# A two-layer graph network: layer 1 computed as (scaled h)ᵀ·adjᵀ first and W last

## The reference

```python
h = relu(layernorm(x))
# layer 0: attention over adj, three powers
Xw = h @ Wv + bv;  sj = Xw @ aw[:d, 0];  si = Xw @ aw[d:, 0]
e = leaky_relu(sj[:, None, :] + si[:, :, None] + ab[0], 0.2)
alpha = adj * exp(e);  T = alpha / (sum(alpha, -1) + 1e-12)
H = sum_k ((T^k h) @ Wk[k] + bk[k]),  k = 0, 1, 2
x = x + relu(H)
# layer 1
h = relu(layernorm(x))
Ah = adj + eye;  dh = rsqrt(sum(Ah, -1))
x = x + relu((dh * Ah * dh) @ h @ W + bias)
```

## Time and profile before

| | us |
|---|---|
| median of 3 runs | 801.88 (801.55 to 802.0) |
| the profiled execution | 801.45 |
| its span | 799.5 |
| TensorE busy | 784.4 (98%) |
| VectorE busy | 638.6 (80%) |
| ScalarE busy | 515.5 (64%) |
| GpSimd busy | 129.4 (16%) |
| granted TensorE clock | 0.998 of full |

### The profile page before, as it was taken

How to read it: one execution, slowest core, us unless ns; L and a number is a source line. 1 busy time by engine, 2 the same in 40 slices (tenths; PEclk the granted TensorE clock), 3 DMA queues, 4 the chain that set the end, 5 groups by cost and what they waited for, 6 DMA issues and landing times.

```text
span 799.5 us, 15983 instructions
## 1 busy us (share of the span) xinstructions
PE 784.4 (98%) x6142; PEld 756.0 (95%) x6142; DVE 638.6 (80%) x1544; ACT 515.5 (64%) x987; POOL 129.4 (16%) x120
## 2 busy tenths in 40 slices
PE   8798999999999999999999999999999999999998
PEld 8597999989999899998999999999999999999998
DVE  6985889868897688976989679896798868895676
ACT  3986766757576676666667567665776657667142
POOL 1032010311104111030201402023010220103200
PEclk9999999999999999999999999999999999999999
DMA  7555435843278251772527625284343842356403
GB/s 240 221 156 170 139 117 177 274 144 134 66 224 295 75 171 54 244 258 67 194 70 250 214 73 192 75 297 156 126 140 128 287 127 99 100 182 234 158 9 106
DMA packets 64492, 128.71 MB, mean 161 GB/s; under 512 B 5536, under 2 KB 31520, under 8 KB 64416
## 3 DMA queue, kind: packets, MB, share of 16 engines
q1 hardware_dynamic: 55648, 97.01, 37.1%
q10 hardware_dynamic: 8768, 30.68, 11.5%
HBM read 119.28 MB, written 8.39 MB: 160 GB/s over the span
## 4 chain that ended last, share of the span: by engine, by line
PE 91%; ACT 4%; DVE 4%; issue 1%; DMA 0%; POOL 0%; SPq 0%; DVEq 0%; ACTq 0%
PE acc L1029 22%; PE acc L1031 22%; PE acc L1030 22%; PE da L904 13%; PE db L904 6%; PE tp L896 3%; ACT tg_e L393 1%; PE acc L924 1%; ACT t_hi L407 1%; ACT tg_e L399 1%; DVE h L587 1%; DMA h<-x_dram 0%; DVE g_tmp L677 0%; DVE ht_lo L606 0%; ACT a_raw L424 0%
## 5 line engine op out<-in xcount | busy, mean ns | idle before, releaser
L1029 PE MATMUL acc<-g_hi,t_hi 128*128 128x256 f32 (+1 forms) x1024 | 293.0, 286 | 2.7 <-DVE g_lo L632 2.7
L1031 PE MATMUL acc<-g_hi,t_lo 128*128 128x256 f32 (+1 forms) x1024 | 289.9, 283 | 0.0
L1030 PE MATMUL acc<-g_lo,t_hi 128*128 128x256 f32 x1024 | 288.7, 282 | 0.0
L1029 PEld LDWEIGHTS acc<-g_hi,t_hi 128*128 128x128 f32 x1024 | 193.9, 189 | 3.1 <-issue 3.1
L1030 PEld LDWEIGHTS acc<-g_lo,t_hi 128*128 128x128 f32 x1024 | 194.3, 190 | 0.0
L1031 PEld LDWEIGHTS acc<-g_hi,t_lo 128*128 128x128 f32 x1024 | 194.1, 190 | 0.0
L1029 PE MATMUL acc<-g_hi,a_hi 128*128 128x256 f32 x512 | 145.5, 284 | 0.1
L1030 PE MATMUL acc<-g_lo,a_hi 128*128 128x256 f32 x512 | 144.0, 281 | 0.0
L1031 PE MATMUL acc<-g_hi,a_lo 128*128 128x256 f32 x512 | 144.0, 281 | 0.0
L327 POOL TENSOR_TENSOR g_lo<-g_tmp,g_hi 128x256 fp32r<-128x256 f32 x64 | 60.6, 947 | 353.0 <-ACT g_hi L449 353.0
L393 ACT ACTIVATE tg_e<-si,sij 128x256 f32<-128x256 f32 x256 | 109.4, 501 | 12.9 <-DVE t_lo L657 10.2
(11 more groups left out here) (129 smaller groups left out, 1424.3 us busy)
## 6 DMA issues: line engine op xcount, KB each, us to landing
a_raw<-adj_dram SPq DMA_DIRECT2D x64, 512.0 KB, 4.5
a_raw<-adj_t_dram SPq DMA_DIRECT2D x64, 512.0 KB, 4.9
tg_a<-adj_t_dram ACTq DMA_DIRECT2D x58, 512.0 KB, 4.0
x_res<-x_dram SPq DMA_DIRECT2D x64, 128.0 KB, 3.6
out_dram<-o_tile SPq DMA_DIRECT2D x64, 128.0 KB, 3.0
...
```

Source lines behind the costliest of these rows:

```text
L1029: nc.tensor.matmul(acc[:, s, 0:n], l_hi, r_hi, start=(jt == 0), stop=False)
L1030: nc.tensor.matmul(acc[:, s, 0:D], l_hi, r_lo, start=False, stop=False)
L1031: ins = nc.tensor.matmul(acc[:, s, 0:n], l_lo, r_hi, start=False, stop=(jt == NT - 1))
```

## The change

Layer 1 is computed in the other order. The normalised h is scaled by dh first (the factor goes into the power: GpSimd takes ((var + eps) · row sum)^(-1/2), `moments1`), and `hs_high` on ScalarE applies it, with a bias that VectorE makes (`bias1_of`) and relu, into `tmp`, and rounds it to `hs_hi`; `hs_low` on VectorE makes the low part. The tiles of hs are the weights as they lie, so nothing is transposed, and the adjacency moves, 512 columns at a time: `layer1_piece(q)` is six matmuls of 512 columns that add tile q mod 8 of h into the transposed sum of half of the rows, (`zt[0]` for q = 0 to 7, in the banks of `da`; `zt[1]` for q = 8 to 15, in those of `tp`). A second array, `adj_z`, has the adjacency in that order; a chunk of it serves two pieces. When eight pieces are summed, zt is split (`zt_high`, `zt_low`, into `ht_hi` and `ht_lo`) and is the weights of the product with W, `out_product`, six matmuls of 256 columns for each tile of rows; `out_chunk` on VectorE finishes it straight from that bank. Products 0 to 3 stand behind pieces 10 to 13, products 4 to 7 behind chunks 1 to 4 of the next batch's U (in the last batch at its end).

Besides: the norm of layer 0 moves from VectorE to ScalarE (`norm0`, with `bias0`), h of a batch is loaded in four parts, each once the pieces no longer read the space it shares with `hs_hi`, the diagonal is two instructions for each of four chunks instead of one for each of eight, and the tables of T's units are new.

```diff
-    LEAKY_Z, EXP_Z = {0: 5, 4: 6, 6: 7}, {0: 5, 5: 6, 6: 7}
-    HIGH_Z, HIGH_U = {3: 4, 5: 5}, {0: 6, 1: 7}
+    LOW_V = {1: 0, 2: 1, 6: 2}
+    LEAKY_Z, EXP_Z = {3: 5, 6: 6, 11: 7}, {4: 5, 7: 6, 12: 7}
+    HIGH_Z, HIGH_U = {0: 3, 5: 4, 9: 5, 13: 6}, {0: 7}
...
+    OUT_Z = {10 + i: i for i in range(HJ)}
+    OUT_U = {1 + i: HJ + i for i in range(HJ)}
...
+            def load_h0(b, g):
+                if b > 1:
+                    sp.wait_ge(piece_done, (b - 2) * NP + NT + 2 * g + 2)
+                else:
+                    sp.wait_ge(tp0_full, NG)
+                sp.dma_start(h0[:, 2 * g:2 * g + 2, :], x_v[b, :, 2 * g:2 * g + 2]).then_inc(x0_loaded[g], 16)
...
+            def hs_high(b, par, g):
+                act.wait_ge(nb1_ready, b * NG + g + 1)
+                if g > 0:
+                    act.wait_ge(hs_ready, b * NT + 2 * g)
+                for t in (2 * g, 2 * g + 1):
+                    nc.scalar.activation(tmp[:, t % 2, :], p0[:, par, t, :], ACT.Relu, bias=nb1[:, t:t + 1],
+                                         scale=rstd1[:, t:t + 1]).then_inc(h1_ready, 1)
+                for t in (2 * g, 2 * g + 1):
+                    act.wait_ge(h1_ready, b * NT + t + 1)
+                    nc.scalar.copy(hs_hi[:, t, :], tmp[:, t % 2, :]).then_inc(hs_hi_done, 1)
+            def zt_high(b, r):
+                for f in range(KD):
+                    if f == KD - 1:
+                        act.wait_ge(piece_done, b * NP + (r + 1) * NT)
+                    else:
+                        act.wait_ge(zt_full, 2 * b + r + 1)
+                    nc.scalar.copy(zt_hi[:, f, :], zt[r][:, f, :]).then_inc(zt_hi_done, 1)
...
-                    l1_scaled(b, 2 * g)
-                    l1_scaled(b, 2 * g + 1)
-                        a_round(b, *A_FIRST[i])
...
+                for q in range(NP):
+                    if q == NP // 2:
+                        zt_high(b, 0)
+                    if q + 4 < NP:
+                        a_round(b, (q + 4) // 2, q % 2)
+                    if q == 1:
+                        hs_high(b, par, NG - 1)
+                    if not last:
+                        if q in HIGH_Z:
+                            t_high(b + 1, HIGH_Z[q], b + 2 == B)
+                        if q in LEAKY_Z:
+                            leaky(b + 1, LEAKY_Z[q])
+                        if q in EXP_Z:
+                            exponent(b + 1, EXP_Z[q])
...
+                nc.vector.scalar_tensor_tensor(out=ve1[:, c], in0=mv1[:, c, 1], scalar=EPS_LN, in1=row_a1[:, c],
+                                               op0=ALU.add, op1=ALU.mult).then_inc(ve1_ready, 1)
...
+            def hs_low(b, g):
+                for t in (2 * g, 2 * g + 1):
+                    dve.wait_ge(hs_hi_done, b * NT + t + 1)
+                    nc.vector.tensor_tensor(hs_lo[:, t, :], tmp[:, t % 2, :], hs_hi[:, t, :].bitcast(F32),
+                                            ALU.subtract).then_inc(hs_ready, 1)
+            def zt_low(b, r):
+                for f in range(KD):
+                    dve.wait_ge(zt_hi_done, (2 * b + r) * KD + f + 1)
+                    nc.vector.tensor_tensor(zt_lo[:, f, :], zt[r][:, f, :], zt_hi[:, f, :].bitcast(F32),
+                                            ALU.subtract).then_inc(zt_ready, 1)
+            def out_chunk(b, par, i):
                 s = i % 2
 
-                dve.wait_ge(acc_full, b * PHASES + 2 * NT + i + 1)
-                nc.vector.scalar_tensor_tensor(out=z_tmp[:, s, :], in0=acc[:, acc_slot(Z_PHASE, i), 0:D], scalar=dh[:, i:i + 1],
+                dve.wait_ge(out_full, b * NT + i + 1)
+                if i == 0:
+                    dve.wait_ge(dh_ready, b + 1)
+                dve.wait_ge(stored[s], 16 * (b * (NT // 2) + i // 2 + 1))
+                nc.vector.scalar_tensor_tensor(out=o_tile[:, s, :], in0=out_bank[i % OB][:, 0:D], scalar=dh[:, i:i + 1],
                                                in1=bias1[:, :], op0=ALU.mult, op1=ALU.add).then_inc(z_tmp_done, 1)
-                dve.wait_ge(z_tmp_done, b * NT + i + 3)
-
-                dve.wait_ge(stored[s], 16 * (b * (NT // 2) + i // 2 + 1))
-                nc.vector.scalar_tensor_tensor(out=o_tile[:, s, :], in0=z_tmp[:, s, :], scalar=0.0,
+                dve.wait_ge(z_tmp_done, b * NT + i + 1)
+                nc.vector.scalar_tensor_tensor(out=o_tile[:, s, :], in0=o_tile[:, s, :], scalar=0.0,
                                                in1=p0[:, par, i, :], op0=ALU.max, op1=ALU.add).then_inc(o_ready, 1)
...
-                        moments(b * NG + i // 2 + 1, st1, mv1, ve1, stats1, mean1, ve1_ready, (i - 1, i))
+                        moments1(b, i // 2)
+                        if i > 1:
+                            hs_low(b, i // 2 - 1)
                     elif i > 0:
-                        norm1(b, par, i // 2 - 1)
-                    if i == 6:
-                        transposed_lo(1, ht1_hi_done, b, ht1_ready)
+                        bias1_of(b, i // 2 - 1)
...
+                for q in range(NP):
+                    if q == NP // 2:
+                        zt_low(b, 0)
+                    if q + 4 < NP:
+                        a_low(b, (q + 4) // 2, q % 2)
+                    if q == 0:
+                        bias1_of(b, NG - 1)
+                    if q == 3:
+                        hs_low(b, NG - 1)
+                    if q - 1 in OUT_Z:
+                        out_chunk(b, par, OUT_Z[q - 1])
+                    if q in DIAG_Z:
+                        diag(b, DIAG_Z[q])
+                    if not last:
+                        if q in PROD_Z:
+                            t_prod(b + 1, PROD_Z[q])
+                        if q in LOW_Z:
+                            t_low(b + 1, LOW_Z[q])
...
-            def layer1_transposes(b, g):
-
-                pe.wait_ge(h1_ready, b * NT + 2 * g + 2)
-                transposes(g, lambda g, s: h1[:, g % 2, s, :], tp1_full)
-
...
+            def layer1_piece(b, q):
+                i, h = q // 2, q % 2
+                r, jt = i // HJ, q % NT
+                pe.wait_ge(a_ready[h], b * NT + NT + i + 1)
+                if r == 0:
+                    pe.wait_ge(hs_ready, b * NT + jt + 1)
+                a = slice(h * HJ, (h + 1) * HJ)
+                r_hi, r_lo = (part[:, i % 2, a].rearrange("p q i -> p (q i)") for part in (a_hi, a_lo))
+                for f in range(KD):
+                    l_hi, l_lo = hs_hi[:, jt, f * P:(f + 1) * P], hs_lo[:, jt, f * P:(f + 1) * P]
+                    nc.tensor.matmul(zt[r][:, f, :], l_hi, r_hi, start=(jt == 0), stop=False)
+                    nc.tensor.matmul(zt[r][:, f, :], l_hi, r_lo, start=False, stop=False)
+                    ins = nc.tensor.matmul(zt[r][:, f, :], l_lo, r_hi, start=False, stop=(jt == NT - 1))
+                    if f == KD - 1:
+                        ins.then_inc(piece_done, 1)
+                    elif jt == NT - 1:
+                        ins.then_inc(zt_full, 1)
+            def out_product(b, t):
+                pe.wait_ge(zt_ready, KD * (2 * b + t // HJ + 1))
+                if t >= OB:
+                    pe.wait_ge(z_tmp_done, b * NT + t - OB + 1)
+                c = slice(t % HJ * P, (t % HJ + 1) * P)
+                split_product(out_bank[t % OB], D, [(zt_hi[:, f, c], zt_lo[:, f, c], wl_hi[:, f, :], wl_lo[:, f, :])
+                                                    for f in range(KD)]).then_inc(out_full, 1)
...
+                    if i in OUT_U and b > 0:
+                        out_product(b - 1, OUT_U[i])
```

More of the change, by code:

```diff
@@ L283, in batch @@
                         load_chunk(b, i)
-                for i in range(RS, NT):
-                    stores(b, i - RS)
-                    if i == RS:
-                        load_chunk(b, RS + 2)
-                        load_chunk(b, RS + 3)
-                for i in range(NT - RS, NT):
-                    if left > 0:
-                        rows(b + 1, (i - NT + RS,))
-                    stores(b, i)
-            load_h0(1)
+                load_chunk(b, RS + 2)
+                load_chunk(b, RS + 3)
+                if left > 0:
+                    rows(b + 1, (0, 1))
+                for g in range(NG):
+                    if left > 1:
+                        load_h0(b + 2, g)
+                    if g < 2 and left > 0:
+                        rows(b + 1, (g + 2,))
+                    if g == 1:
+                        stores(b, 0)
+                        stores(b, 1)
+                    if g == 2:
+                        stores(b, 2)
+                        stores(b, 3)
+            for g in range(NG):
+                load_h0(1, g)
             rows(0, range(RS))
@@ L304, in _ @@
             batch(B - 1, 0)
+            for i in range(HJ, NT):
+                stores(B - 1, i)
             for s in range(2):
@@ L332, in batch @@
                     g1_split(b, i)
-                    if i == 4 and not last:
+                    if i == 3 and not last:
```

(28 more changed lines are left out.)

315 lines of the change are left out of this document (132 added, 183 removed).

## The result

The changed kernel takes 804.19 us (median of 6 runs, 803.01 to 805.74), the kernel before 801.67 (801.55 to 802.00): a ratio of 1.0033, 95% interval 1.0020 to 1.0047. It is slower, by 2.5 us; I had forecast 801.0, the gain and the new wait cancelling. The profiled execution took 805.74 us, its span is 803.1.

A forecast was written before the change was run, and what follows sets the result against it. TensorE, busy 98% of the span, was taken as the bound. 801.45 - 19.0 (its saved work) + 18.9 (waits at product 0) - 0.8 = 800.5, plus 0.4 to the median, say 801; range 792 to 808, the forecast case's own 797 to 804.

The forecast's parts named there:

- My own sign of being wrong: Pieces at another pitch, a wait of TensorE inside U or V, or zt ready before piece 10 ends.
- TensorE's work: Transposes, narrow matmuls and small gaps go from layer 1: TensorE saves 2.72 us a batch.
- the chain: ScalarE and VectorE work up to product 0 in layer 1: TensorE waits 2.7 us in seven batches.
- T0: Start of layer 1's first piece on TensorE; product 0 is reached 15.35 us later.
- so I price this at nothing: VectorE, waiting for chunk 0's store, starts U about 1.2 us late: nothing, or 1 us a batch.
- the 2.2 of the tail: Store time at the kernel's end, from the end of the last chunk, 797.3, to 799.5: 2.2 us.
- the norms on ScalarE: Layer 0 norms, 0.8 a pair, in U and layer 0 products: nothing, or at worst 0.8 a batch.
- The last batch: Longer end after the last piece, 9.7 us; from V's start 57.9 against 57.2, 0.7 lost.
- Rival two: Slower: VectorE bounds from V on; with 1 us more lag the wait is 3.7 a batch, 808; chance 0.28.
- Rival one: Shorter chain before product 0: 1.1 to 2.0 us of wait, 1.5 in its sum, 792.6; chance 0.24.
- Rival three: Full gain: ScalarE runs ahead and product 0 in layer 1 never waits, 782; chance 0.06.

The follow-up runs named there:

- e4: Changed kernel with three output tiles and the load of row 3 behind the stores of chunks 0 and 1: 799.92 us.
- e5: e4 with, in the first batch alone, the norms of tiles 0 to 3 back on VectorE: 798.01 us.
- e6: e4 with the last norm's bias ahead of VectorE's low part of adjacency chunk 2: 794.88 us.
- e8: e4 with ScalarE's rounding of Z ahead of unit 6's Exp, VectorE's low part of Z ahead of a_low, chunk 6's diagonal one piece earlier: 794.54 us.
- e7: Changed kernel with e4, e5, e6 and e8 together: 787.15 us, ratio 0.9821 to the kernel before.
- e2: Changed kernel with three output tiles in place of two: 800.30 us, ratio 0.9981 to the kernel before.
- e2b: Changed kernel, two output tiles, with the 512 KB load of row 3 behind the stores of chunks 0 and 1: 800.59 us, ratio 0.9985 to the kernel before.
- e12: Kernel before with two extra 1.05 us copies on ScalarE ahead of the first batch's row sums of tiles 5 and 6: 803.70 us, ratio 1.0023.

## Why the prediction was wrong

The mechanism and the two large terms were right; two terms that I had priced at nothing were worth 6.2 us together (4.3 by e4, 1.9 by e5). My own sign of being wrong, a wait of TensorE inside U, is there: 1.62 us before product 4.

- **TensorE's work, -2.72 a batch, and the chain, +2.7.** Right. V fell by 0.84; L by 2.2, with the 2.85 that moved into U. Product 0 started at T0 + 17.68 (forecast 18.05), so by starts the chain costs 17.68 - 15.35 = 2.3 a batch and not 2.7; the rows show 0.45 of it at piece 6 (forecast 0.8) and 1.46 at product 0. ScalarE idled 1.23 before the last norms where I had 1.5 to 2: the bias was there at T0 + 4.96 and not at 5.4. From there to `zt_high` it had no idle time, as forecast. That this chain binds is shown: 0.6 off its head gave 0.6 a batch (e6), Z put first on both engines gave 0.95 a batch (e8), and both together add up (e7).
- **The failing step: "so I price this at nothing; if U's slack is used up it is 1 us a batch".** The slack was used up. I had let VectorE start U 1.2 us late; here it started 4.6 after U's first block was done (340.26 against 332.85 + 24 x 0.1188 = 335.70), because I took the store at about the 2.2 of the tail, where behind 512 KB it took 4.5 to 6.2 in batches 0 to 5, and because I counted only TensorE's three accumulators as cover, and not product 4, which TensorE has behind U's second block. It came to 0.2 to 1.9 us a batch, 0.6 in the mean. Worth 3.5 us in the profiled execution, 4.3 in the medians (804.2 to 799.9, e4); e2 and e2b show that it is the store.
- **The second failing step: the norms on ScalarE, "nothing, or at worst 0.8 a batch".** It was worked out for the steady batches, and there it holds: D is 18.71 in all six. The first batch's U has less room, as the windows of the kernel before show (U of batches 0 and 2, at the end of this section; the fourth busy figure is ScalarE's): 23.05 us of 28.30 against 15.78 of 23.79. It was worth 2.85 us in the profiled execution, which had the low clock too, and 1.9 in the medians by e5; and e12 shows that idle time there alone, without the change, costs 2.1.
- **Without both, the forecast would have been too high:** e5 is 798.0 against my 801, its profiled execution 798.8 against 800.5. Of these 1.7 us, 7 x 0.17 = 1.2 are the shorter chain in L; I had also added 0.4 for the step from the profiled execution to the median, which in e5 is 0.8 the other way.
- **The last batch.** +3.32 of +3.5. Right.
- **The rivals.** Rival two had the sign and named the store wait, but put the price on VectorE's lag in V; V is 23.0 us and no wait stands in it. Rival one's 1.5 a batch did not come. Rival three's full gain was not reached even by e7, which still waits 0.5 a batch. What I lacked was the first batch as a case of its own; the stretches I priced were of the later ones.

```profile
38.40:66.70 28.30, 25.84 (x200) 25.38 (x200) 21.36 (x53) 23.05 (x42) 9.10 (x8) 0.94 0.57 175
236.97:260.76 23.79, 23.79 (x203) 23.79 (x201) 18.58 (x52) 15.78 (x30) 8.31 (x8) 1.00 0.87 290
```
